# Fourier neural layer with spline network: mixing products over 128 rows, inverse products over 64 rows, and a quarter of the mixing weights loaded one block later

## The chip, the cores and the metric

One NeuronCore of a Trainium2 chip runs the whole kernel in one launch. The metric is the device time of that launch in microseconds; lower is better. All data are fp32.

## What is computed

The input x has 16 images of 64 channels, 128 x 128. It is group-normed (32 groups of two channels), then goes through a spectral convolution plus a 1 x 1 convolution, two layers of a spline network (KAN) over the channels and a GELU, and is added to x:

```python
def spectral_conv2d(x, w1, w2):
    x_ft = jnp.fft.rfft2(x)
    out_ft = zeros((b, c, h, w // 2 + 1), complex64)
    out_ft[:, :, :16, :16]  = einsum('bixy,ioxy->boxy', x_ft[:, :, :16, :16],  w1)
    out_ft[:, :, -16:, :16] = einsum('bixy,ioxy->boxy', x_ft[:, :, -16:, :16], w2)
    return jnp.fft.irfft2(out_ft, s=(h, w))

g = group_norm(x)
y = spectral_conv2d(g, w1, w2) + einsum('bchw,oc->bohw', g, conv_w) + conv_b
y = kan_linear(kan_linear(y as tokens, k1), k2)        # silu product + 8 spline bases
out = x + gelu(y)
```

Only 32 x 16 frequencies of each image are kept (32 values of kx, 16 of ky). Each has its own complex 64 x 64 matrix: w1 and w2 are, as real and imaginary parts, four arrays of 64 x 64 x 16 x 16, 4 MB each.

## The kernel before

The work is done in four blocks; at the end of a block all engines wait for one another, and an engine's program in a block includes what it issues as DMA.

**Forward** (`forward`, L237). For each image TensorE transforms along h (L381), turns the planes (L390) and transforms along w (L402); ScalarE and VectorE evict, and VectorE takes the statistics of the raw image (L355). SP loads the images in eight groups of channels. The kept frequencies of all images stay in SBUF as `modes`: partitions are 64 channels for each of two halves, a half holding eight of the sixteen x of a group. A group g is the lower (w1) or the upper (w2) kx. Behind the last image SP issues the loads of w1's real and imaginary parts (L337, `load_mix_weights`, L133: 8 DMAs of 512 KB a part, in runs of 512 bytes). The buffer `big` has room for all four parts, but w2's parts lie where the images are, so they are issued in the next block.

**Statistics and mixing** (`statistics_and_mix`, L474). SP issues the pick table (L533) and w2's two parts. A chain of small VectorE instructions and three groups of TensorE products gives mean and reciprocal deviation of every image and channel. Then, for both groups g and the eight x of a half: VectorE multiplies the frequencies by the reciprocal deviation into `normed` (two instructions, L664 and L667: -imag, real, imag), TensorE multiplies `normed` by the weights of 16 ky in two parts (L569: 64 products of 64 rows, 32 stationary columns and 64 moving ones, spread over 2 row halves and 4 column tiles), ScalarE evicts (L590), and issues two stores of 128 KB to the scratch `modes_dram` (L595). `normed`, `mixed` and the accumulators have two buffers each. TensorE's program is written out for all 16 x; an fp32 product is two records each of weight load and matmul in the trace. Before a group TensorE waits for its two weight parts (L559).

**Inverse along h** (`inverse_rows`, L673). For each pair of images SP loads the mixed frequencies (`spec`, L705: four DMAs a pair, in runs of 1 KB), TensorE makes 4 products of 512 columns for each of the two images (L756), ScalarE evicts one image and VectorE the other, and SP stores 1 MB of rows for each (L710). Both images of a pair lie in `spec`, in 64 partitions each. The product of one of them runs over all 128 rows, with a table (`inv_h_sb[u]`) whose other 64 rows VectorE has set to zero (L780). SP also loads the first two tiles of the next block here.

**Second half** (`second_half`, L784). 128 tiles of 1024 columns for a pair of images: the inverse along w and the 1 x 1 convolution (L1032, L1040), two spline layers of 14 products each (L1053), with ScalarE and VectorE making their inputs, GELU, and the addition of x by DMA. Tiles run in a loop of two.

The lines that matter most:

```python
for half in range(2):                          # L567, mixing before
    ky, own = col * MIX_Q + at, slice(half * C, (half + 1) * C)
    ins = nc.tensor.matmul(
        ps[u][col * MIX_M:(col + 1) * MIX_M, half, at * C:(at + 1) * C],
        normed[u][own, ky, 1 - part:3 - part, :].rearrange("p r b -> p (r b)"),
        mix_w[g][part][own, :, x, ky], ..., tile_position=(half * C, col * MIX_M))
```

## Time and profile before

| what | value |
|---|---|
| median of 3 runs | 3799.74 us (3797.88 to 3802.43) |
| profiled execution | 3802.58 us |
| its span, first to last instruction | 3800.8 us |
| busy: TensorE, VectorE, ScalarE | 96%, 92%, 89% |
| mean granted TensorE clock | 0.986 |
| DMA | 328.76 MB, 86 GB/s over the span |

The page divides the span into 40 slices of 95 us. Forward fills the first two and most of the third; statistics, mixing and inverse lie in the third to fifth, up to 463 us; the rest is the second half. In the timeline a row is: start in us, us, engine, line, operation, out<-in with shapes, count, and in brackets the idle time of the engine before it with what ended it ("issue": nothing that the profile shows). SPq and ACTq rows are DMA issues.

### The profile page before, as it was taken

Reading aid. Unit: us, or ns where it says so; the run is one execution under the profiler, and the core shown is the slowest. Engines: PE = TensorE matmul, PEld = TensorE weight load, DVE = VectorE, ACT = ScalarE, POOL = GpSimd, SP = SyncE. Lnnn points to the kernel's source line nnn. Section 1 sums busy time; section 2 is a strip of 40 time slices with the busy share of each in tenths; the row PEclk is TensorE's granted clock in tenths of the full one; section 3 lists DMA queues with packets and bytes.
Section 4 is the critical chain, followed back from the end, with each engine's and each line's share of the span. In section 5 each row is a group of like instructions: output and inputs, shape, how many; then the busy total and the mean of one; then the engine's idle time right before and its main releaser. Section 6 shows DMA issues by size and latency. Waiting matters only on the chain.

```text
span 3800.8 us, 103324 instructions
## 1 busy us (share of the span) xinstructions
PE 3658.0 (96%) x38188; PEld 1573.7 (41%) x38188; DVE 3505.1 (92%) x3882; ACT 3391.6 (89%) x3509; POOL 110.8 (3%) x132
## 2 busy tenths in 40 slices
PE   8974699999999999999999999999999999999997
PEld 4433334444444444444444444444444444444444
DVE  7752299999999999999999999999999999999996
ACT  4531299999999999999999999999999999999996
POOL 0000000000000000000000000000000000000000
PEclk9987899999999999999999999999999999999999
DMA  9997723223223223223322322322322322332231
GB/s 260 290 248 140 236 51 72 58 68 72 61 64 72 66 60 72 66 59 72 70 58 69 72 59 67 72 62 64 72 65 60 72 66 59 72 71 58 69 72 45
DMA packets 327425, 328.76 MB, mean 86 GB/s; under 512 B 87120, under 2 KB 259664, under 8 KB 325328
## 3 DMA queue, kind: packets, MB, share of 16 engines
q1 hardware_dynamic: 304336, 256.73, 25.2%
q0 software_dynamic: 18432, 67.12, 10.9%
q10 hardware_dynamic: 4608, 4.20, 0.4%
q8 instruction: 38, 0.62, 0.1%
q14 instruction: 11, 0.09, 0.0%
HBM read 239.88 MB, written 88.08 MB: 86 GB/s over the span
## 4 chain that ended last, share of the span: by engine, by line
PE 86%; DVE 0%; issue 0%; ACT 0%; POOL 0%; POOLq 0%; ACTq 0%; DVEq 0%
PE l_ps L1053 81%; PE y_ps L1040 3%; PE y_ps L1032 3%; DVE cube2l L929 0%; DVE cube3r L929 0%; ACT above L968 0%; ACT offset L983 0%; ACT size L979 0%; ACT S L972 0%; ACT below L976 0%; DVE cube1r L929 0%; DVE cube1l L929 0%; DVE cube0l L929 0%; ACT L972 0%; DVE cube0r L929 0%
## 5 line engine op out<-in xcount | busy, mean ns | idle before, releaser
L983 ACT ACTIVATE offset<-size 128x1024 f32<-128x1024 f32 x1280 | 1240.4, 1044 | 8.2
L929 DVE SCALAR_TENSOR_TENSOR cube0r<-below,offset 128x1024 f32<-128x1024 f32 x256 | 312.4, 1220 | 58.1 <-ACT offset L983 57.5
L929 DVE SCALAR_TENSOR_TENSOR cube0l<-above,offset 128x1024 f32<-128x1024 f32 x256 | 311.5, 1217 | 0.0
L929 DVE SCALAR_TENSOR_TENSOR cube1r<-below,offset 128x1024 f32<-128x1024 f32 x256 | 311.4, 1216 | 0.0
L929 DVE SCALAR_TENSOR_TENSOR cube1l<-above,offset 128x1024 f32<-128x1024 f32 x256 | 311.3, 1216 | 0.0
L929 DVE SCALAR_TENSOR_TENSOR cube3r<-below,offset 128x1024 f32<-128x1024 f32 x256 | 311.3, 1216 | 0.0
L929 DVE SCALAR_TENSOR_TENSOR cube2l<-above,offset 128x1024 f32<-128x1024 f32 x256 | 311.2, 1216 | 0.0
L929 DVE SCALAR_TENSOR_TENSOR cube2r<-below,offset 128x1024 f32<-128x1024 f32 x256 | 311.2, 1216 | 0.0
L938 DVE SCALAR_TENSOR_TENSOR inner_cube<-below,square 128x1024 f32<-128x1024 f32 x256 | 311.2, 1216 | 0.0
L929 DVE SCALAR_TENSOR_TENSOR cube4r<-below,offset 128x1024 f32<-128x1024 f32 x256 | 311.2, 1215 | 0.0
L929 DVE SCALAR_TENSOR_TENSOR cube3l<-above,offset 128x1024 f32<-128x1024 f32 x256 | 311.1, 1215 | 0.0
L929 DVE SCALAR_TENSOR_TENSOR cube4l<-above,offset 128x1024 f32<-128x1024 f32 x256 | 311.1, 1215 | 0.0
L1053 PE MATMUL l_ps<-S,turned_w 64*64 64x512 f32 x2048 | 273.6, 591 | 7.8 <-issue 7.8
L979 ACT ACTIVATE size<-below 128x1024 f32<-128x1024 f32 x256 | 271.2, 1059 | 8.1
L1053 PE MATMUL l_ps<-cube3r,turned_w 64*64 64x512 f32 x2048 | 273.6, 589 | 0.9 <-DVE cube3r L929 0.9
L1053 PE MATMUL l_ps<-cube1l,turned_w 64*64 64x512 f32 x2048 | 273.9, 589 | 0.0
L1053 PE MATMUL l_ps<-cube2l,turned_w 64*64 64x512 f32 x2048 | 273.6, 589 | 0.1
L1053 PE MATMUL l_ps<-cube4r,turned_w 64*64 64x512 f32 x2048 | 273.6, 589 | 0.1
L1053 PE MATMUL l_ps<-cube3l,turned_w 64*64 64x512 f32 x2048 | 273.6, 589 | 0.1
L1053 PE MATMUL l_ps<-cube2r,turned_w 64*64 64x512 f32 x2048 | 273.6, 589 | 0.0
L1053 PE MATMUL l_ps<-cube4l,turned_w 64*64 64x512 f32 x2048 | 273.5, 589 | 0.1
L1053 PE MATMUL l_ps<-cube1r,turned_w 64*64 64x512 f32 x2048 | 273.3, 589 | 0.1
(120 smaller groups left out, 6020.2 us busy)
## 6 DMA issues: line engine op xcount, KB each, us to landing
big<-in_x_dram SPq DMA_DIRECT2D x128, 512.0 KB, 7.0
x_ring<-in_x_dram SPq DMA_DIRECT2D x256, 256.0 KB, 4.0
act_out<-in_x_dram POOLq DMA_DIRECT2D x128, 512.0 KB, 7.1
out_dram<-act_out SPq DMA_DIRECT2D x128, 512.0 KB, 2.7
rows_scratch<-rows SPq DMA_DIRECT2D x16, 1024.0 KB, 6.0
rows_t<-rows_scratch SPq DMA_DIRECT2D x512, 32.0 KB, 5.6
big<-in_spec_w_r_dram SPq DMA_DIRECT2D x16, 512.0 KB, 11.1
big<-in_spec_w_i_dram SPq DMA_DIRECT2D x16, 512.0 KB, 11.1
```

What stands on the lines that cost most here:

```text
L929: nc.vector.scalar_tensor_tensor(out=cube[q][side][:], in0=distance[layer][:], scalar=EDGE - KNOTS[q], in1=offset[layer][q][:], op0=ALU.mi ...
L938: nc.vector.scalar_tensor_tensor(out=inner_cube[:], in0=below[layer][:], scalar=EDGE, in1=square[layer][:], op0=ALU.subtract, op1=ALU.mult ...
L979: nc.scalar.activation(size[layer][:], below[layer][:], ACT.Abs, bias=EDGE, scale=-1.0).then_inc(size_ready[layer], 1)
L983: nc.scalar.activation(offset[layer][q][:], size[layer][:], ACT.Square, bias=-KNOTS[q]).then_inc(offset_ready[layer], 1)
L1032: nc.tensor.matmul(y_ps[image, n * MM:(n + 1) * MM], conv_t[par][half, image], src[half, i * MM:(i + 1) * MM], start=True, stop=False, ski ...
L1040: ins = nc.tensor.matmul(y_ps[image, at:at + W], rows[half, par, h, :], inv_w_sb[half, i, :], start=False, stop=(h == HH - 1), skip_group_ ...
L1053: ins = nc.tensor.matmul(dst[cols, r * MM:(r + 1) * MM], kan_w[layer][rows_, f, :], src[rows_, n * MM:(n + 1) * MM], start=(f == 0), stop= ...
```

## The change

Three parts, with the layouts that go with them.

1. SP issues only w1's real part at the end of the forward block. The imaginary part is issued in the block of statistics and mixing, after the pick table and ahead of w2.
2. A mixing product now reads all 128 rows: `normed` gets a third axis for the half, and the scales `rs_own` and `rs_neg`, zero in the rows of the other half, make the stationary operand (64 columns: two of -imag/real/imag, two halves, 16 images) block-diagonal. There are 32 products for an x, of 128 rows, 64 stationary and 64 moving columns, on two column tiles. VectorE makes `normed` with three multiplies of 512 elements instead of one of 512 and one of 256, and clears the scales once (L610 before). `mixed` gets buffers of its own, and the stores go out in runs of 2 KB instead of 1 KB.
3. In the inverse, one table lies in both halves of the partitions; the product of image u reads only its 64 rows, at tile position (64 u, 0). Nothing is zeroed. `modes_dram` is laid out so that an image's frequencies are loaded in one DMA of 64 rows of 4 KB, two DMAs for a pair.

The tables are permuted to match (columns of `dft_w`, rows of `inv_h`), with the same sizes.

```diff
-            for part in range(2):
-                load_mix_weights(sp, t, weights[:, 2 + part], 0, part)
+            load_mix_weights(sp, t, weights[:, 2], 0, 0)
...
             sp.dma_start(pick_sb[:], t["pick"]).then_inc(pick_loaded, 16)
-            for part in range(2):
-                load_mix_weights(sp, t, mix_w[1][part], 1, part)
+            for g, part in ((0, 1), (1, 0), (1, 1)):
+                load_mix_weights(sp, t, mix_w[g][part], g, part)
...
-                            for col in range(4):
-                                for half in range(2):
-                                    ky, own = col * MIX_Q + at, slice(half * C, (half + 1) * C)
-                                    ins = nc.tensor.matmul(
-                                        ps[u][col * MIX_M:(col + 1) * MIX_M, half, at * C:(at + 1) * C],
-                                        normed[u][own, ky, 1 - part:3 - part, :].rearrange("p r b -> p (r b)"),
-                                        mix_w[g][part][own, :, x, ky], start=(part == 0), stop=(part == 1),
-                                        skip_group_check=True, tile_position=(half * C, col * MIX_M))
+                            for col in range(2):
+                                ky = col * MIX_Q + at
+                                ins = nc.tensor.matmul(
+                                    ps[u][col * C:(col + 1) * C, at * C:(at + 1) * C],
+                                    normed[u][:, ky, 1 - part:3 - part, :, :].rearrange("p f h b -> p (f h b)"), mix_w[g][part][:, :, x, ky],
+                                    start=(part == 0), stop=(part == 1), skip_group_check=True,
+                                    tile_position=(0, col * C))
...
-                        for half in range(2):
-                            n = x + (SH * half if g == 0 else 2 * MODES - SH * (half + 1))
-                            nc.scalar.dma_start(modes_dram[bass.ds(n, 1)].rearrange("n l r b f -> (n l r b) f"),
-                                                mixed[u][:, half, :]).then_inc(stored[u], 16)
+                        for col in range(2):
+                            dst = modes_dram[bass.ds(x + SH * g, 1), :, :, :, col, :]
+                            nc.scalar.dma_start(dst.rearrange("s r h b f -> (s r h b) f"),
+                                                mixed[u][col * C:(col + 1) * C, :]).then_inc(stored[u], 16)
...
-                        nc.vector.tensor_tensor(
-                            normed[u][:, :, 1:3, :].rearrange("p k r b -> p r k b"), here,
-                            rs_signed[:, 0:1, :].unsqueeze(2).to_broadcast([P, 2, MODES, B]), ALU.mult)
-                        nc.vector.tensor_tensor(
-                            normed[u][:, :, 0:1, :].rearrange("p k r b -> p r k b"), here[:, 1:2],
-                            rs_signed[:, 1:2, :].unsqueeze(2).to_broadcast([P, 1, MODES, B]),
-                            ALU.mult).then_inc(normed_ready, 1)
+                        for f, part, scale in ((0, 1, rs_neg), (1, 0, rs_own), (2, 1, rs_own)):
+                            ins = nc.vector.tensor_tensor(
+                                normed[u][:, :, f, :, :], here[:, :, part:part + 1, :].to_broadcast([P, MODES, 2, B]),
+                                scale[:].unsqueeze(1).to_broadcast([P, MODES, 2, B]), ALU.mult)
+                        ins.then_inc(normed_ready, 1)
...
-                    for r in range(2):
-                        at = u * K + r * 2 * MODES
-                        sp.dma_start(spec[p][at:at + 2 * MODES, :].rearrange("n (l f) -> n l f", l=4),
-                                     modes_dram[:, :, r, bass.ds(2 * pair + u, 1), :].rearrange("n l b f -> n l (b f)"))\
-                          .then_inc(spec_loaded[p], 16)
+                    sp.dma_start(spec[p][u * K:(u + 1) * K, :],
+                                 modes_dram[:, :, :, bass.ds(2 * pair + u, 1)].rearrange("s r h b l f -> (s r h) (b l f)"))\
+                      .then_inc(spec_loaded[p], 16)
...
-                            nc.tensor.matmul(ps[u][k][:], inv_h_sb[u][:, part, :], spec[p][:, cols:cols + MM],
-                                             start=True, stop=True).then_inc(rows_done[u], 1)
+                            own = slice(u * K, (u + 1) * K)
+                            nc.tensor.matmul(ps[u][k][:], inv_h_sb[own, part, :], spec[p][own, cols:cols + MM],
+                                             start=True, stop=True, tile_position=(u * K, 0)).then_inc(rows_done[u], 1)
...
-            for u in range(2):
-                other = slice((1 - u) * K, (2 - u) * K)
-                nc.vector.memset(inv_h_sb[u][other], 0.0).then_inc(inv_h_zero, 1)
```

## Rows read from the trace of the kernel before

**Rows 1.** The page: its first line, and the instruction queue's packets, MB, share.
```profile
span 3800.8 us, 103324 instructions
...
q8 instruction: 38, 0.62, 0.1%
```

**Rows 2.** Chain that ended last, second half: start us, us, what.
```profile
575.04 24.03 PE l_ps L1053 x224
...
600.80 24.03 PE l_ps L1053 x224
```

**Rows 3.** Timeline of SP's queue: the weight loads and the pick table.
```profile
239.93 19.46 SPq L141 DMA_DIRECT2D big<-in_spec_w_r_dram  x8
...
259.43 21.56 SPq L141 DMA_DIRECT2D big<-in_spec_w_i_dram  x8
281.63 2.00 SPq L533 DMA_DIRECT2D pick_sb<-pick_dram  x1
...
302.66 22.68 SPq L141 DMA_DIRECT2D big<-in_spec_w_i_dram  x8
```

**Rows 4.** Timeline: first statistics matmuls, two scalings, first mixing matmuls.
```profile
282.10 3.93 PE L541 MATMUL ps_mean<-stats,avg 128*128 128x512 f32 x4 [23.78 <-DVE avg_sq L611]
...
302.27 0.69 DVE L664 TENSOR_TENSOR stats<-modes,rs_signed 128x512 f32<-128x512 f32 x1 [0.33 <-DVE modes L654]
...
302.88 0.42 DVE L667 TENSOR_TENSOR stats<-modes,rs_signed 128x256 f32<-128x256 f32 x1
...
303.56 3.13 PE L569 MATMUL mix_ps<-big,stats 64*32 64x64 f32 x202 [3.05 <-DVE stats L667]
```

**Rows 5.** Windows: length, busy of PE, PEld, DVE, ACT, POOL; PEclk, DMA share, GB/s.
```profile
260.00:270.00 10.00, 0.00 (x0) 0.00 (x0) 0.00 (x0) 0.00 (x0) 0.00 (x0) 0.51 1.21 195
...
332.00:334.00 2.00, 0.00 (x0) 0.00 (x0) 0.00 (x0) 0.00 (x0) 0.00 (x0) 1.00 0.32 89
```

**Rows 6.** Timeline of TensorE while mixing: four of the bursts.
```profile
320.27 2.11 PE L569 MATMUL mix_ps<-big,stats 64*32 64x64 f32 x128 [6.78 <-issue]
...
364.21 2.06 PE L569 MATMUL mix_ps<-big,stats 64*32 64x64 f32 x127 [1.75 <-issue]
...
368.05 2.06 PE L569 MATMUL mix_ps<-big,stats 64*32 64x64 f32 x128 [1.77 <-issue]
...
375.72 1.12 PE L569 MATMUL mix_ps<-big,stats 64*32 64x64 f32 x62 [1.76 <-issue]
```

**Rows 7.** DMA queues from 340 to 376 us: packets, MB, share.
```profile
q8 instruction: 9, 0.15, 2.0%
```

**Rows 8.** Timeline of TensorE: one image's transform along w.
```profile
237.06 2.32 PE L402 MATMUL along_w<-dft_w_sb,freq 128*64 128x64 f32 x70
```

**Rows 9.** Line 595, the stores of mixed frequencies: from issue to landing.
```profile
DMA to landing us min/median/max: 1.7/1.7/8.0
```

**Rows 10.** Timeline of the inverse stage and the second half's first instruction.
```profile
380.51 1.13 SPq L714 DMA_DIRECT2D inv_h_sb<-inv_h_dram  x2
...
386.58 15.68 PE L756 MATMUL rows_ps<-spec,inv_h_sb 128*128 128x512 f32 x32 [9.74 <-DMA spec<-modes_scratch]
...
395.35 1.28 SPq L710 DMA_DIRECT2D rows_scratch<-rows  x2
...
439.35 7.13 PE L756 MATMUL rows_ps<-spec,inv_h_sb 128*128 128x512 f32 x16 [2.31 <-DMA spec<-modes_scratch]
...
454.61 0.91 SPq L710 DMA_DIRECT2D rows_scratch<-rows  x2
...
463.23 0.17 DVE L913 COPY consts<-pair_bias 128x2 f32<-128x2 f32 x1 [8.23 <-PEq L677]
```

**Rows 11.** Windows of the inverse stage, columns as in rows 5.
```profile
386.00:463.00 77.00, 58.45 (x128) 24.39 (x128) 22.13 (x32) 19.11 (x32) 0.00 (x0) 0.94 0.86 282
...
405.00:407.00 2.00, 1.58 (x4) 0.87 (x5) 0.00 (x0) 0.42 (x1) 0.00 (x0) 1.00 1.02 430
```

More of the change, by code:

```diff
@@ L43 @@
 MIX_O = 16
-MIX_M = 2 * B
-MIX_Q = MODES // 4
+MIX_Q = MODES // 2
 PAIRS = B // 2
@@ L66, in tables @@
     c, s = np.cos(aw), np.sin(aw)
-    dft_w = np.stack([np.concatenate([c, -s, c, -s], 1), np.concatenate([-s, -c, s, c], 1)], 1)
+    of_cos = np.stack([c, -s], 2).reshape(W, 2 * MODES)
+    of_sin = np.stack([s, c], 2).reshape(W, 2 * MODES)
+    dft_w = np.stack([np.concatenate([of_cos, of_cos], 1), np.concatenate([-of_sin, of_sin], 1)], 1)
     kx = np.concatenate([np.arange(MODES), np.arange(-MODES, 0)]).astype(np.float64)
+    kx = np.concatenate([kx[:MODES].reshape(2, SH).T.ravel(), kx[MODES:].reshape(2, SH)[::-1].T.ravel()])
     ai = 2 * np.pi * np.outer(kx, h) / H
     inv_h = np.stack([np.stack([np.cos(ai), np.sin(ai)], 1), np.stack([-np.sin(ai), np.cos(ai)], 1)], 1)
-    inv_h = inv_h.transpose(1, 0, 2, 3).reshape(4 * MODES, 2, H)
+    inv_h = inv_h.reshape(MODES, 2, 2, 2, H).transpose(0, 2, 1, 3, 4).reshape(4 * MODES, 2, H)
     weight = np.where(ky == 0, 1.0, 2.0)[:, None] / (H * W)
@@ L125, in first_half @@
         big = sb("big", [P, 4, C * W])
-        rs_signed = sb("rs_signed", [P, 2, B])
+        rs_own = sb("rs_own", [P, 2, B])
+        rs_neg = sb("rs_neg", [P, 2, B])
         mix_loaded = [[ctx.enter_context(nc.semaphore(f"mix_loaded{g}{part}")) for part in range(2)] for g in range(2)]
-        t = dict(t, modes=modes, stats=stats, big=big, rs_signed=rs_signed, mix_loaded=mix_loaded)
+        t = dict(t, modes=modes, stats=stats, big=big, rs_own=rs_own, rs_neg=rs_neg, mix_loaded=mix_loaded)
         forward(nc, t)
@@ L474, in statistics_and_mix @@
 def statistics_and_mix(nc, t):
-    modes, stats, modes_dram, rs_signed, big = (t[n] for n in ("modes", "stats", "modes_dram", "rs_signed", "big"))
+    modes, stats, modes_dram, rs_own, rs_neg, big = (
+        t[n] for n in ("modes", "stats", "modes_dram", "rs_own", "rs_neg", "big"))
     conv_two, conv_bias, image_rs, pair_bias = t["conv_two"], t["conv_bias"], t["image_rs"], t["pair_bias"]
@@ L514, in statistics_and_mix @@
         var_ready, root_ready, chain = sem("var_ready"), sem("root_ready"), sem("chain")
-        rm_ready, bias_done = sem("rm_ready"), sem("bias_done")
+        rm_ready, bias_done, rs_clear = sem("rm_ready"), sem("bias_done"), sem("rs_clear")
         parts = big[:].rearrange("p i (o x k) -> p i o x k", x=SH, k=MODES)
         mix_w = [[parts[:, 2], parts[:, 3]], [parts[:, 0], parts[:, 1]]]
-        NRM, MXD = MODES * 3 * B, 2 * MIX_Q * C
+        NRM = MODES * 3 * 2 * B
         spare = stats[:].rearrange("p b g k -> p (b g k)")
-        normed = [spare[:, u * NRM:(u + 1) * NRM].rearrange("p (k r b) -> p k r b", r=3, b=B) for u in range(2)]
-        mixed = [spare[:, 2 * NRM + u * MXD:2 * NRM + (u + 1) * MXD].rearrange("p (h f) -> p h f", h=2)
-                 for u in range(2)]
-        ps = [ctx.enter_context(nc.psum_tensor(f"mix_ps{u}", [P, 2, MM], F32)) for u in range(2)]
+        normed = [spare[:, u * NRM:(u + 1) * NRM].rearrange("p (k f h b) -> p k f h b", f=3, h=2, b=B) for u in range(2)]
+        mixed = [sb(f"mixed{u}", [P, MIX_Q * C]) for u in range(2)]
+        ps = [ctx.enter_context(nc.psum_tensor(f"mix_ps{u}", [P, MIX_Q * C], F32)) for u in range(2)]
         normed_ready, mix_done, mix_kept = sem("normed_ready"), sem("mix_done"), sem("mix_kept")
@@ L608, in link @@
                 dve.wait_ge(chain, links[0])
+            nc.vector.memset(rs_own[:], 0.0).then_inc(rs_clear, 1)
+            nc.vector.memset(rs_neg[:], 0.0).then_inc(rs_clear, 1)
             nc.vector.memset(avg[:], 0.5 / P).then_inc(set_up, 1)
@@ L650, in _ @@
             link(nc.vector.tensor_scalar(pair_bias[:, :, 1], pair_bias[:, :, 0], EDGE, None, ALU.add))
-            link(nc.vector.tensor_copy(rs_signed[:, 0, :], rs_c[:]))
-            link(nc.vector.tensor_scalar(rs_signed[:, 1, :], rs_c[:], -1.0, None, ALU.mult))
+            dve.wait_ge(rs_clear, 2)
+            for half in range(2):
+                own = slice(half * C, (half + 1) * C)
+                nc.vector.tensor_copy(rs_own[own, half, :], rs_c[own, :])
+                link(nc.vector.tensor_scalar(rs_neg[own, half, :], rs_c[own, :], -1.0, None, ALU.mult))
             dc = modes[0:C, 0, 0, 0, :]
@@ L662, in _ @@
                         dve.wait_ge(mix_done, 2 * x2 + (SH * g + u + 1))
[L663 to L670 removed]
+                        here = modes[:, bass.ds(place_, 1), g, :, :].rearrange("p s (k r) b -> p (s k) r b", r=2)
+                        for f, part, scale in ((0, 1, rs_neg), (1, 0, rs_own), (2, 1, rs_own)):
[3 more added lines that the diff above has]
+                        ins.then_inc(normed_ready, 1)
 def inverse_rows(nc, t):
@@ L685, in inverse_rows @@
         BANKS = 2 * MODES * C // MM
-        inv_h_sb = [sb(f"inv_h_sb{u}", [2 * K, 2, H]) for u in range(2)]
+        inv_h_sb = sb("inv_h_sb", [2 * K, 2, H])
         spec = [sb(f"spec{p}", [2 * K, MODES * C]) for p in range(2)]
@@ L691, in inverse_rows @@
               for u in range(2)]
[L692 removed]
+        inv_h_loaded = sem("inv_h_loaded")
         spec_loaded = [sem(f"spec_loaded{p}") for p in range(2)]
@@ L749, in _ @@
                     pair = 2 * pair2 + p
-                    pe.wait_ge(spec_loaded[p], 64 * (pair2 + 1))
+                    pe.wait_ge(spec_loaded[p], 32 * (pair2 + 1))
                     for k in range(BANKS):
```

9 lines of the change are left out of this document (3 added, 6 removed).

## The prediction

> **What bounds the kernel now.** I read the page first, then the chain of waits, then the timeline stage by stage. The span is 3800.8 us [rows 1]. In the chain of waits the second half is TensorE alone: one tile's products start at 575.04 and the next tile's at 600.80, so 25.76 us a tile, for 128 tiles some 3300 us [rows 2]. The change touches none of that. What it can move is the time at which the second half starts, 463.23 us [rows 10]. Whatever the first 463 us lose or gain arrives at the end one for one, since the chain of the second half holds nothing that was ready earlier. So I look for what ends last in each stage before 463.
>
> *Weights.* SP issues the first weights behind the last images, real part until 259.39, imaginary part until 280.99, each issue some 2.6 us, and only then does the block end: SP's first issue of the next block is at 281.63 and the statistics' first matmul at 282.10 [rows 3, 4]. From 260 on no engine works and the DMA engines run full, 195 GB/s [rows 5]. The second weights are issued until 325.34 [rows 3], and the queue is empty from about 332.5: the stretch 332 to 334 has a DMA share of 0.32 [rows 5]. So the 16 MB of weights are one unbroken stream from 240 to 332.5.
>
> *Mixing.* It starts at 303.56 [rows 4] and ends at 376.84 (375.72 + 1.12), 73.3 us for 16 values of x. But a burst of 128 matmuls, one x, takes only 2.1 us; then TensorE idles with no releaser: 6.78 us before the burst at 320.27, while weights stream, and 1.77 us before that at 368.05, when they don't. Two quiet bursts are 3.84 us apart [rows 6]. The 128 matmul and 128 weight-load records of a burst have a counterpart in the instruction queue: 9 packets, 0.15 MB, in the 36 us from 340 to 376, where some 9.5 bursts fall [rows 7]. So one packet of 16 KB comes for each burst: mixing waits for its own code, at 3.84 us a packet when the DMA is quiet and 8 to 9 us when it is full.
>
> *Inverse.* SP begins it at 380.51; the first product starts at 386.58, the first pair of stores is issued at 395.35, the last at 454.61, and the second half's first instruction follows at 463.23. That is 8.47 us a pair of images (59.26 / 7). The products of one pair take 7.13 us, and TensorE then waits 2.31 us for a spec load [rows 10]. The DMA averages 282 GB/s over the stage but reaches 430 in a stretch that is nearly all stores [rows 11]. So the loop is load, product, store, with DMA and TensorE covering each other only in part.
>
> **The change, part by part.**
>
> *Half of the first weights issued later.* The first block now ends when SP is done with the real part, at about 260, not 281.6. The stream of 32 issues keeps its order, with the pick table between the parts, and stays limited by the DMA: its end stays near 332.5. The imaginary part, 8 issues from about 262 to 283.5, lands near 292 (the last issue of the second weights starts at 325.34 less 2.6 and the queue is empty 10 us later) [rows 3, 5]. The statistics, 21.5 us from 282.10 to 303.56 [rows 4], run from about 260.7 to 282, beside the stream. So mixing of the first group starts at 292 instead of 303.6: it waits for weights, no longer for statistics. SP's only other work that is moved past is the pick table, issued ahead of the imaginary part, 2.00 us [rows 3], needed by VectorE only 8 us later. Two more memsets and two more small VectorE instructions cost under 1 us and lie under that wait for weights: nothing.
>
> *Mixing over 128 rows.* An x has 32 products instead of 64, so 64 matmul and 64 weight-load records: one 16 KB packet of code for two x. This form, 128 rows by 64 columns with 64 moving, exists already: the second transform runs 70 records in 2.32 us, 33 ns each [rows 8], so 64 take 2.1 us. Array work is not saved (half of the stationary operand is zero now); code is. VectorE has three multiplies of 512 elements per x; two in a row start 0.61 us apart, and one takes 0.69 [rows 4], so 1.9 us plus some 0.35 us of signals: 2.3 us an x, beside TensorE. I take 2.3 us an x.
>
> First group: 8 x under the full DMA. Code costs 8.5 / 2 = 4.3 us an x, and the ScalarE stores, which land in up to 8.0 us [rows 9] with two buffers, cost 4 us. The first three x have their code (the first burst now is 202 matmuls [rows 4]), so it ends at about 292 + 7 + 5 x 4.3 = 321. That is before the second weights land, so it is off the path. All 2 MB of its results now go out under the stream, 1 MB more than before, when four of the eight x were done by 332; at the 195 to 280 GB/s of that stretch I add 2.5 us: second weights landed at 335.
> Second group: 8 x 2.3 = 18.4 us. What one packet costs in two x is unseen: nothing if it is fetched beside 4.6 us of work (3.84 is less), 1.77 if not; four packets, 0 to 7 us; I take 1, since the first three x have code waiting. The clock: TensorE idled from 321 to 335, and idle stretches stand at a granted clock of 0.51, the 1.2 GHz level [rows 5]; the slow level on the first x costs 0 to 3 us, I take 2. Mixing ends at 335 + 21.4 = 356.4 instead of 376.8: **20.4 us** gained. Bounds: 332.5 + 17 = 349.5 (27 gained) to 338 + 28 = 366 (11 gained).
>
> *Inverse over 64 rows.* Each image's product reads 64 rows, and the two images of a pair have different row halves. No row shows two 64 x 128 tiles side by side. Lower bound of the products: halved, 3.6 us a pair; upper: 7.13, one after the other. The nearest rows are the second half's 64 x 64 tiles: 8 records in 0.86 us (224 in 24.03) [rows 2], against 0.44 us each (7.13 / 16) for full tiles [rows 10], so four tiles overlap, row halves among them. I take 3.6. Spec loads are 16 issues with 4 KB pieces instead of 32 with 1 KB: same bytes, which relieves SP. The zeroing of unused halves goes; it was hidden by the spec load.
> Then DMA is the bound: 2 MB of stores and 0.5 MB of spec per pair, 2.6 MB, 6.1 us at 430 GB/s (9.3 at the mean of 282, but that has the idle time in it). Turnaround matters: after a spec load lands, products, eviction (1) and latency (about 2) follow, 6.6 us. I take 7.0 us a pair. First store: the first product comes about 1 us earlier, and pair 0, at first at the slow clock, takes 6 us instead of 8.8: 3.8 us less. Seven periods: 7 x 1.47 = 10.3 us less. The two tile loads at the end stay. Together **14 us**. Bounds: 3 (clock at its slow level all through, as TensorE is busy only half of the time, so 7 us a pair again) to 19 (6.2 us a pair and nothing lost).
>
> **Sum:** 20.4 + 14 = 34.4 us. The profiled execution took 3802.58 us (span plus 1.8), so 3768.2; the median of the three runs is 2.8 lower, 3799.74, and gives **3765 us**, 0.9% faster. A difference of 0.2%, 7.6 us, is what a measurement of this kernel can tell from none.
>
> **A rule against it.** The idle of 1.77 us comes once in 256 instructions [rows 6, 7]: that is what the rows show, and the sum goes by it: half of the code, half of the fetches. If the idle belonged to the x instead, the sum would be that of rival 1. The Trainium skill, Runtime: NRT & Kernel Launch, section on instruction fetch mechanics, agrees on blocks of 256 instructions, but says that the cost of crossing one is mostly hidden, since the next is fetched while the current one runs; by that rule the idle has another cause, and halving the code brings nothing. The trace shows the idle, so it does not hide here; which of the two it is, the trace leaves to rival 1.
>
> **Rivals.**
> 1. *The mixing pace stays at 3.84 us an x*, because the idle belongs to the x (buffers, results, stores), not to its code. For it: bursts are also exactly one x. Against it: the first burst of 202 crosses an x without idle [rows 4]. Mixing ends at 335 + 8 x 3.84 = 366; 11 + 14 = 25 us gained: 3775. Chance 0.12.
> 2. *The row halves don't overlap, or the clock drops*: a pair stays at 7 us of TensorE. Inverse gains 3: 23 us in all, 3776. For it: no such tile in the trace, and 0.5 clock levels wherever TensorE idles. Against it: [rows 2]. Chance 0.2; both rivals together, 14 us gained, 3786, chance 0.04.
> 3. *Nothing measurable*: the two stages are held by their transfers after all (weights landing later under 2 MB of stores, stores at 250 GB/s). Gains under 7.6 us: about 3797. Chance 0.03.
> 4. *Slower*: the code after the mixing lies elsewhere in memory, and the second half's loop of two tiles (1056 matmul and weight-load instructions) may no longer be held whole. One fetch a turn at the 1.77 us of [rows 6], 62 turns, is 110 us lost against 34 gained: 3876. It decides from 0.55 us a turn on. Against it: in the whole span the instruction queue moved 38 packets [rows 1], so this loop is fetched once, and its place before was not special. Chance 0.02. The Trainium skill, same page and section, says that a taken branch to a target outside the window forces such a fetch; no run here shows it.
> The forecast itself: 0.59, alone 3757 to 3774.
>
> **Range.** 3752 to 3784: the forecast with its bounds, and rivals 1 and 2. Faster by over 0.2%: 0.94; within: 0.03; slower: 0.03.
>
> **What would show it.** Right: the statistics' first matmul near 261; SP's last weight issue still near 325; the first mixing burst near 292; the second group from about 335 at 2.3 us an x, idle without releaser at most once in two x; mixing done by 357; 64-row products with 3.6 us a pair; DMA share near 1 through the inverse; first instruction of the second half near 429; 25.76 us a tile after it. Wrong: mixing bursts 3.8 us apart per x (1), 7 us of products a pair or a clock of 0.5 in the inverse (2), an idle per turn in the second half (4).

## The result, and the profile after

The changed kernel takes 3785.9 us (median of 6 runs, 3780.91 to 3787.38), beside 3800.87 us for the kernel before in the same 6 rounds: a ratio of 0.9957, 95% interval 0.9947 to 0.9967. It is faster by 15 us, where 35 were forecast, and lies 1.9 us above the range. The profiled execution took 3786.73 us with a span of 3784.9. Each trace below is of one execution.

The second half is what it was: in the chain of waits one tile's products start at 533.50 and the next tile's at 559.27, 25.77 us a tile [rows 2]. So the 15.5 us are all gained before its first instruction, at 447.75 instead of 463.23. Here is SP's queue in the timeline of the changed kernel, and under it the mixing on TensorE:

```profile
259.56 1.99 SPq L539 DMA_DIRECT2D pick_sb<-pick_dram  x1
261.60 18.98 SPq L147 DMA_DIRECT2D big<-in_spec_w_i_dram  x8
280.62 21.82 SPq L147 DMA_DIRECT2D big<-in_spec_w_r_dram  x8
302.48 24.43 SPq L147 DMA_DIRECT2D big<-in_spec_w_i_dram  x8
```

```profile
260.12 3.82 PE L547 MATMUL ps_mean<-stats,avg 128*128 128x512 f32 x4 [2.45 <-DVE avg_sq L618]
...
288.95 21.98 PE L574 MATMUL mix_ps<-big,stats 128*64 128x64 f32 x384 [10.13 <-DMA big<-in_spec_w_i_dram]
...
312.48 7.36 PE L574 MATMUL mix_ps<-big,stats 128*64 128x64 f32 x128 [1.55 <-ACT mixed L595]
...
335.87 28.84 PE L574 MATMUL mix_ps<-big,stats 128*64 128x64 f32 x512 [16.03 <-DMA big<-in_spec_w_i_dram]
```

The block changes at 259.6, the statistics run beside the weights, the last weight is issued at 326.9 (302.48 + 24.43; 325.3 before), and the second group starts at 335.87, when its weights have landed. All of that is as forecast. The new thing is the last row: 512 records in 28.84 us, 56.3 ns each, without a gap. Before, bursts of 16 ns a record stood between idle times [rows 6]; now TensorE is busy all the time at a slower pace, 3.6 us an x instead of 3.84. Mixing ends at 364.71 instead of 376.84.

So the 12.1 us gained there hardly come from the pace of the second group. They come from how much is left when the last weights land. Three more bursts of the kernel before, beside those of [rows 4, 6]:

```profile
311.41 2.08 PE L569 MATMUL mix_ps<-big,stats 64*32 64x64 f32 x127 [4.72 <-issue]
...
328.31 2.13 PE L569 MATMUL mix_ps<-big,stats 64*32 64x64 f32 x127 [5.93 <-issue]
...
334.14 2.08 PE L569 MATMUL mix_ps<-big,stats 64*32 64x64 f32 x128 [3.71 <-issue]
```

Ahead of the burst at 334.14 it had made 202 + 127 + 128 + 127 = 584 records, four and a half x, so eleven and a half were left, 42.7 us of them. The changed kernel has its whole first group done at 319.84 and eight x left, 28.84 us. The code did halve: from 300 to 378 us the instruction queue moved 16 packets (0.26 MB) before, from 286 to 366 us 8 (0.13 MB) after.

The inverse in the same timeline, with four of the seven waits for a spec load, the pairs of stores around them, and the first instruction of the second half:

```profile
375.25 8.87 PE L763 MATMUL rows_ps<-spec,inv_h_sb 64*128 64x512 f32 x32 [10.53 <-DMA spec<-modes_scratch]
...
381.49 0.92 SPq L717 DMA_DIRECT2D rows_scratch<-rows  x2
...
391.43 5.87 PE L763 MATMUL rows_ps<-spec,inv_h_sb 64*128 64x512 f32 x16 [7.32 <-DMA spec<-modes_scratch]
...
398.12 0.87 SPq L717 DMA_DIRECT2D rows_scratch<-rows  x2
...
398.67 3.70 PE L763 MATMUL rows_ps<-spec,inv_h_sb 64*128 64x512 f32 x16 [1.36 <-DMA spec<-modes_scratch]
...
407.98 6.13 PE L763 MATMUL rows_ps<-spec,inv_h_sb 64*128 64x512 f32 x16 [5.61 <-DMA spec<-modes_scratch]
...
414.93 0.88 SPq L717 DMA_DIRECT2D rows_scratch<-rows  x2
...
439.26 0.91 SPq L717 DMA_DIRECT2D rows_scratch<-rows  x2
...
447.75 0.17 DVE L917 COPY consts<-pair_bias 128x2 f32<-128x2 f32 x1 [11.31 <-PEq L685]
```

The products of a pair do take about half of the 7.13 us of [rows 10], 3.70 us, when the clock is up. But every other pair comes after 5.6 to 7.3 us of idle and takes 5.9 to 6.3. The stores of a pair are 8.25 us apart on average ((439.26 - 381.49) / 7), against 8.47. The stage, which starts at 368.98, takes 78.8 us instead of 82.7.

The account of the 15.5 us: mixing 12.1, less 0.6 more between its end and the inverse, inverse 3.95. The last term is the least certain. In e1, e3, e5 and e6 below the inverse is that of the changed kernel, and its stage takes 80.8, 80.8, 81.3 and 79.4 us where this profile has 78.8; with 128-row products it takes 82.7 here, 82.7 in e7 and 82.9 in e9. By these profiles the 64-row inverse is worth 1.4 to 3.95 us.

### The profile page after: what moved, and what is told of

Its sections match the earlier page's. It is cut to its first block, busy times and chain, and to the rows that moved or that the text cites. A ratio compares the mean times of both kernels' runs of the same rounds, so it can differ in the third digit from the quotient of the medians.

```text
span 3784.9 us, 101254 instructions
## 1 busy us (share of the span) xinstructions
PE 3662.3 (97%) x37164; PEld 2765.6 (73%) x37164; DVE 3518.6 (93%) x3900; ACT 3391.7 (90%) x3509; POOL 110.9 (3%) x132
## 4 chain that ended last, share of the span: by engine, by line
PE 87%; DVE 0%; issue 0%; ACT 0%; POOL 0%; POOLq 0%; ACTq 0%; DVEq 0%
PE l_ps L1057 82%; PE y_ps L1044 3%; PE y_ps L1036 2%; DVE cube2l L933 0%; DVE cube3r L933 0%; ACT above L972 0%; ACT size L983 0%; ACT offset L987 0%; ACT S L976 0%; ACT below L980 0%; DVE cube1r L933 0%; DVE cube1l L933 0%; DVE cube0l L933 0%; ACT L976 0%; DVE cube0r L933 0%
## 5 line engine op out<-in xcount | busy, mean ns | idle before, releaser
L1057 PE MATMUL l_ps<-S,turned_w 64*64 64x512 f32 x2048 | 330.5, 592 | 8.1 <-issue 8.1
L1057 PE MATMUL l_ps<-cube1l,turned_w 64*64 64x512 f32 x2048 | 330.0, 589 | 1.0 <-issue 1.0
L1057 PE MATMUL l_ps<-cube0r,turned_w 64*64 64x512 f32 x2048 | 329.9, 591 | 0.6 <-DVE cube0r L933 0.6
L1057 PE MATMUL l_ps<-cube3r,turned_w 64*64 64x512 f32 x2048 | 329.7, 589 | 0.8 <-DVE cube3r L933 0.8
L1057 PE MATMUL l_ps<-below,turned_w 64*64 64x512 f32 x2048 | 329.9, 591 | 0.0
L1057 PE MATMUL l_ps<-cube4r,turned_w 64*64 64x512 f32 x2048 | 329.7, 589 | 0.1
L1057 PE MATMUL l_ps<-cube4l,turned_w 64*64 64x512 f32 x2048 | 329.7, 589 | 0.1
L1057 PE MATMUL l_ps<-bowl,turned_w 64*64 64x512 f32 x2048 | 329.6, 589 | 0.0
L1057 PE MATMUL l_ps<-inner_cube,turned_w 64*64 64x512 f32 x2048 | 329.6, 589 | 0.0
L1057 PE MATMUL l_ps<-cube0l,turned_w 64*64 64x512 f32 x2048 | 329.1, 590 | 0.0
```

The costliest lines, as they stand in the source:

```text
L1057: ins = nc.tensor.matmul(dst[cols, r * MM:(r + 1) * MM], kan_w[layer][rows_, f, :], src[rows_, n * MM:(n + 1) * MM], start=(f == 0), stop= ...
```

## The experiments

Two questions. Why does a mixing record take 56 ns, when the same form takes 33 ns in the transform along w [rows 8]? And why does the inverse hardly gain from half the TensorE time? A third: which part of the change is worth what. The times of the kernels timed in rounds, as ratios to the kernel before in the same job:

| run | median us | ratio, 95% interval |
|---|---|---|
| changed kernel | 3785.9 | 0.9957, 0.9947 to 0.9967 |
| e1 moving operand contiguous | 3778.3 | 0.9938, 0.9921 to 0.9954 |
| e2 loads before stores | 3782.4 | 0.9951, 0.9935 to 0.9968 |
| e3 all of w1 in forward | 3788.9 | 0.9962, 0.9948 to 0.9977 |
| e7 products over 128 rows | 3791.0 | 0.9973, 0.9964 to 0.9983 |
| e8 four spec buffers | 3777.8 | 0.9934, 0.9917 to 0.9951 |
| e9 kernel before, move alone | 3797.7 | 0.9992, 0.9983 to 1.0002 |
| e11 e8, early real products | 3773.1 | 0.9922, 0.9908 to 0.9936 |
| e12 e11, one start flag | 3772.3 | 0.9923, 0.9909 to 0.9936 |

All differences are under 1% of the total. The intervals of e1, e2, e3, e7 and e8 overlap that of the changed kernel, so what sets them apart from it is read from their traces; those of e11 and e12 don't overlap it.

### The pace of the mixing products

**e1**, neighbouring values:

```diff
-  normed[u][:, ky, ...], mix_w[g][part][:, :, x, ky],
+  normed[u][:, ky, ...], big[:, (2 if g == 0 else 0) + part, (x * MODES + ky) * C:(x * MODES + ky + 1) * C],
```

> The changed kernel with one edit: the moving operand of each mixing product is 64 neighbouring values of the weight buffer instead of 64 values 512 bytes apart (other weights, same count, same waits). Theory S (the strided read of the moving operand sets the pace of 56 ns a record): records at about 33 ns as in the transform along w, so an x at 2.1 to 2.3 us instead of 3.6, the second group in 17 to 19 us instead of 28.8, total about 10 us lower, near 3776. Theory C (code fetch still sets the pace, 256 instructions in 7.2 us): unchanged, 28.8 us. Theory W (weight loads of 64 columns over 128 rows do not overlap): unchanged, 28.8 us.

The second group in its timeline:

```profile
335.40 5.52 PE L574 MATMUL mix_ps<-big,stats 128*64 128x64 f32 x128 [17.77 <-DMA big<-in_spec_w_i_dram]
341.19 3.95 PE L574 MATMUL mix_ps<-big,stats 128*64 128x64 f32 x128 [0.27 <-DVE stats L675]
...
349.65 2.08 PE L574 MATMUL mix_ps<-big,stats 128*64 128x64 f32 x64 [0.28 <-DVE stats L675]
352.33 2.24 PE L574 MATMUL mix_ps<-big,stats 128*64 128x64 f32 x64 [0.59 <-ACT mixed L595]
```

An x takes 2.08 us, 32.5 ns a record, and the group 19.2 us. Where it now waits, it waits for VectorE and for ScalarE's evictions. Theory S holds; code fetch and weight loads, which the edit leaves alone, don't set the pace of the second group. The low clock after the idle shows here: granted 0.50 from 335 to 337 and 0.53 from 337 to 339, the first two x take 5.52 us instead of 3.95. Mixing ends 10.1 us earlier, but 2.4 us more pass between its end and the inverse, and the total fell by 7.6 us by the medians.

**e5** and **e6**: is it the power of two, or the step as such?

```diff
-  mix_w[g][part][:, :, x, ky],
+  big[:, ..., x * MODES + ky:x * MODES + ky + 63 * 127 + 1:127],             # e5: 508 bytes
+  big[:, ..., (x * MODES + ky) * 60:(x * MODES + ky) * 60 + 127:2],          # e6: 8 bytes
```

> The changed kernel with the moving values of each mixing product 508 bytes apart instead of 512 (other weights). If the power of two is what slows the strided read: about 33 ns a record, the second group in 17 to 19 us. If any step beyond a short line is slow (the Trainium skill, SBUF - State Buffer, has a note on lines of 16 bytes): unchanged, 56 ns a record and 28.8 us.

> The changed kernel with the moving values 8 bytes apart (other weights). If the step costs as such: 56 ns a record, 28.8 us for the second group. If two values in 16 bytes are enough (same note): as fast as neighbouring values, 33 ns a record, 19 us.

The second group of e5, then of e6 (timelines):

```profile
335.46 30.29 PE L574 MATMUL mix_ps<-big,stats 128*64 128x64 f32 x512 [15.03 <-DMA big<-in_spec_w_i_dram]
```

```profile
336.29 18.54 PE L574 MATMUL mix_ps<-big,stats 128*64 128x64 f32 x512 [15.40 <-DMA big<-in_spec_w_i_dram]
```

508 bytes is as slow as 512 (59 ns a record), 8 bytes as fast as none (36 ns, with the waits). One execution of each gave 3790.6 and 3779.6 us. So it is not the power of two, and not a step as such. That is as far as the runs go: why the far values are slow stays open, and steps between 8 and 508 bytes weren't tried. The Trainium skill, SBUF - State Buffer, section Door 1: The DMA port swizzle, has a note that fits: SBUF is read in lines of 16 bytes, full speed needs two hits in a line. At 8 bytes of step there are two fp32 values in 16 bytes, at 508 one.

Why did the kernel before not show it? It read with the same step. But it had four column tiles and two row halves: a record came every 16.3 ns (2.08 / 128), so each of the eight tiles took one every 130 ns. The changed kernel has two tiles: one every 113 ns each. A contiguous read, e1, gives 65 ns a tile. So I read it thus: the slow stream was there before, hidden behind eight tiles side by side, and with two it sets the pace. This part is not shown; no run reads neighbouring values on eight tiles.

**e4**, the other half of the account: was it code fetch that paced the kernel before? Its imaginary-part products were left out, so that an x has half the code.

```diff
-                        for part in range(2):
+                        for part in range(1):
...
-                                        mix_w[g][part][own, :, x, ky], start=(part == 0), stop=(part == 1),
+                                        mix_w[g][part][own, :, x, ky], start=True, stop=True,
```

> The kernel before with the real-part products of the mixing alone (the imaginary-part products are left out), so 64 matmul and 64 weight-load records an x. Theory C (in the kernel before, one fetch of 256 instructions sets the pace): idle of 1.8 us once in two x, so a quiet x takes about 1.9 us instead of 3.84. Rival X (the idle belongs to the x): idle at every x, a quiet x takes 1.05 + 1.77 = 2.8 us.

```profile
304.12 2.06 PE L569 MATMUL mix_ps<-big,stats 64*32 64x64 f32 x128 [3.05 <-DVE stats L667]
306.53 1.13 PE L569 MATMUL mix_ps<-big,stats 64*32 64x64 f32 x64 [0.35 <-DVE stats L667]
308.08 0.40 PE L569 MATMUL mix_ps<-big,stats 64*32 64x64 f32 x9 [0.42 <-ACT stats L590]
311.02 1.10 PE L569 MATMUL mix_ps<-big,stats 64*32 64x64 f32 x55 [2.54 <-issue]
...
316.88 0.44 PE L569 MATMUL mix_ps<-big,stats 64*32 64x64 f32 x8 [1.31 <-DVE stats L667]
318.47 1.12 PE L569 MATMUL mix_ps<-big,stats 64*32 64x64 f32 x56 [1.15 <-issue]
...
338.90 1.21 PE L569 MATMUL mix_ps<-big,stats 64*32 64x64 f32 x64 [1.68 <-ACT stats L590]
341.01 1.17 PE L569 MATMUL mix_ps<-big,stats 64*32 64x64 f32 x64 [0.89 <-ACT stats L590]
```

The rows to see are x9 and x55. An x has 64 records, and the idle without releaser stands inside it: after 201 records (128 + 64 + 9), as after the 202 of [rows 4], and again 127 later (55 + 64 + 8). The idle belongs to every 128 matmul records, 256 instructions, wherever an x ends. Rival X, and with it rival 1 of the prediction, falls. The number of theory C was missed, and that of rival X nearly hit: a quiet x takes 2.6 us (five steps from 336.05 to 349.08), not 1.9, because ScalarE, which waits for its stores, is late next; once the weights have landed no idle without releaser is left. And in the changed kernel, where a block of 256 instructions lasts 7.2 us, the fetch is hidden whole. So a fetch costs what it takes longer than the work of a block: 3.84 against 2.1 us before.

The same count stands in the first group of e1, beside the full DMA, where an x again has 64 records but of the 128-row form:

```profile
297.78 0.50 PE L574 MATMUL mix_ps<-big,stats 128*64 128x64 f32 x9 [0.24 <-DVE stats L675]
300.03 1.85 PE L574 MATMUL mix_ps<-big,stats 128*64 128x64 f32 x55 [1.74 <-issue]
```

With 192 records ahead of these rows, the idle stands after 201 again, and once more (0.39 us) 127 later. With the strided read gone, the fetch shows again.

### The inverse

**e2**: the spec loads of pair n+2 ahead of the stores of pair n.

```diff
                     for u in range(2):
                         sp.wait_ge(rows_kept[u], BANKS * pair + 2 * BANKS)
-                        store(pair, p, u)
-                    load(pair + 2, p)
+                    load(pair + 2, p)
+                    for u in range(2):
+                        store(pair, p, u)
```

> The changed kernel with SP's order in the inverse turned round: after a pair is evicted, first the spec loads of the pair after next, then the two stores. Theory L (a loop of latencies: a spec load waits in SP's queue behind 2 MB of stores, products wait for it, stores wait for them): the idle of 5.6 to 7.3 us before every other pair's products shrinks below 1 us, a pair takes 6.3 to 7.0 us instead of 8.25, 9 to 13 us less in all, near 3775. Theory B (the DMA moves no more than this mix allows): under 2 us gained.

```profile
384.65 0.97 SPq L717 DMA_DIRECT2D rows_scratch<-rows  x2
...
433.89 0.91 SPq L717 DMA_DIRECT2D rows_scratch<-rows  x2
```

A pair takes 7.03 us ((433.89 - 384.65) / 7), just above what theory L expected. The stage is 5.8 us shorter (370.27 to 443.20, 72.9 us), but by the medians only 3.5 us were gained, a third of what was expected; the second weights landed 1.3 us later in this profile. The first store now waits for both evictions and the loads, and is issued 8.1 us after the first product instead of 6.2, and four of the six later pairs still have 2.4 to 3.8 us of idle ahead of their products. Theory L is supported, but turning the order round isn't the whole remedy.

**e8**: four spec buffers instead of two, the stores first again.

```diff
-            load(0, 0)
-            load(1, 1)
+            for pair in range(4):
+                load(pair, pair)
...
+            for pair in range(PAIRS - 2):
+                for u in range(2):
+                    sp.wait_ge(rows_kept[u], BANKS * pair + 2 * BANKS)
+                    store(pair, pair % 2, u)
+                if pair + 4 < PAIRS:
+                    load(pair + 4, pair)
...
+                    pe.wait_ge(spec_loaded[p], 32 * (pair4 + 1))
```

> The changed kernel with four spec buffers: four pairs are loaded ahead, then the load of pair n+4 is issued behind the stores of pair n. Theory L: products never wait for a spec load after the first, the DMA is the bound at 340 to 380 GB/s, a pair takes 6.5 to 7.2 us instead of 8.25, and the first stores aren't late as in the run with loads ahead of stores: inverse stage 8 to 12 us shorter, total near 3776. Theory B (DMA bound in any case): under 2 us.

Two product bursts in its timeline; then a window over its stage (length; busy time of PE, PEld, DVE, ACT, POOL; PEclk, DMA share, GB/s), and the same view of the changed kernel:

```profile
398.36 5.49 PE L760 MATMUL rows_ps<-spec,inv_h_sb 64*128 64x512 f32 x16 [1.59 <-DVE rows L774]
405.48 3.70 PE L760 MATMUL rows_ps<-spec,inv_h_sb 64*128 64x512 f32 x14 [1.63 <-DVE rows L774]
```

```profile
384.00:436.00 52.00, 31.57 (x104) 14.13 (x100) 16.99 (x27) 14.53 (x27) 0.00 (x0) 0.80 1.02 375
```

```profile
381.00:440.00 59.00, 32.49 (x112) 12.73 (x108) 19.81 (x29) 17.02 (x29) 0.00 (x0) 0.83 0.93 320
```

Products no longer wait for spec but for VectorE's eviction, which waits for its buffer's store: the DMA is the bound, busy throughout (a share of 1.02) at 375 GB/s instead of 320. TensorE's clock still falls at times (0.80 on the mean); with the DMA busy throughout, that is not what sets the pace. A pair takes 6.80 us ((430.49 - 382.90) / 7, the first and the last pair of stores), the stage 69.8 us, 9 less; the total is 8.1 us lower. Theory L holds, theory B for the changed kernel falls.

**e10**: no spec load after the first two pairs, so that later pairs are computed from the frequencies of pairs 0 and 1.

```diff
-                    load(pair + 2, p)
...
-                    pe.wait_ge(spec_loaded[p], 32 * (pair2 + 1))
+                    pe.wait_ge(spec_loaded[p], 32)
```

> The changed kernel without the spec loads after the first two pairs (later pairs are computed from the frequencies of pairs 0 and 1). Theory L: without the load behind the stores, products are never late, and a pair takes what 2 MB of stores take, 4.9 to 5.4 us at 390 to 430 GB/s, instead of 8.25; 20 us less in all, near 3765. Theory B (stores alone are as slow as the mean of the stage, 320 GB/s): 6.5 us a pair or more.

```profile
388.12 3.78 PE L762 MATMUL rows_ps<-spec,inv_h_sb 64*128 64x512 f32 x16 [0.40 <-DVE rows L776]
393.15 3.79 PE L762 MATMUL rows_ps<-spec,inv_h_sb 64*128 64x512 f32 x16 [1.24 <-DVE rows L776]
```

```profile
380.82 24.67 SPq L717 DMA_DIRECT2D rows_scratch<-rows  x12
...
420.52 0.90 SPq L717 DMA_DIRECT2D rows_scratch<-rows  x2
```

From one pair's products to the next 5.04 us pass for 2 MB of stores, 416 GB/s; one execution gave 3768.1 us. Counted as for the others, over all seven steps and so with the two tile loads at the end, a pair takes 5.67 us ((420.52 - 380.82) / 7). So of the 8.25 us a pair in the changed kernel, 5.7 are stores and tile loads, 1.1 come with the spec bytes beside them (e8), and 1.45 are the loop.

**e7**: the changed kernel with products over 128 rows again (two tables, zeroed halves), its loads and layout kept.

```diff
-                            nc.tensor.matmul(ps[u][k][:], inv_h_sb[own, part, :], spec[p][own, cols:cols + MM],
-                                             start=True, stop=True, tile_position=(u * K, 0)).then_inc(rows_done[u], 1)
+                            nc.tensor.matmul(ps[u][k][:], inv_h_sb[u][:, part, :], spec[p][:, cols:cols + MM],
+                                             start=True, stop=True).then_inc(rows_done[u], 1)
```

> The changed kernel with the 64-row products of the inverse undone (two tables with zeroed halves, products over 128 rows), its loads and layout kept. Theory L (a loop of latencies: products of one pair, then stores and the spec load behind them): two pairs take the products' 7.1 to 8 us plus 10 us, 17 to 18 us instead of 16.6, so 2 to 5 us slower than the changed kernel. If the 64-row products were worth what halving them suggests (3.5 us a pair): 20 us or more slower.

5.1 us slower than the changed kernel by the medians. In the profile the stage runs from 368.01 to 450.70, 82.7 us, that of the kernel before: fewer and larger spec loads are worth nothing that shows, and the gain of the inverse, 3.9 us in these two profiles, is that of the 64-row products. In e7 every pair takes 7.13 us of products, the spec load is late by 2.4 to 3.0 us for every other pair, and the clock stays up.

### Which part is worth what

**e3**: all of w1 issued in the forward block again.

```diff
-            load_mix_weights(sp, t, weights[:, 2], 0, 0)
+            for part in range(2):
+                load_mix_weights(sp, t, weights[:, 2 + part], 0, part)
...
-            for g, part in ((0, 1), (1, 0), (1, 1)):
+            for g, part in ((1, 0), (1, 1)):
```

> The changed kernel with the first part of the change undone: both parts of w1 are issued at the end of the forward block again. Theory H (the second weights' landing at about 335 covers the move): the first group starts at 303.5 instead of 289 and ends at about 335 to 338, the second group follows within 3 us of its weights; 0 to 4 us slower, so 3786 to 3790. Rival (the move is worth its 14 us of earlier start): 10 us or more slower, 3796.

```profile
305.65 21.71 PE L575 MATMUL mix_ps<-big,stats 128*64 128x64 f32 x384 [4.09 <-DVE stats L676]
...
332.64 32.42 PE L575 MATMUL mix_ps<-big,stats 128*64 128x64 f32 x576 [1.16 <-ACT mixed L596]
```

The first group starts 17 us later, and mixing ends at 365.06 instead of 364.71. The move gives 0.35 us of mixing in the traces, 3.0 us between the medians, whose intervals overlap; the inverse, which the edit leaves alone, took 2.0 us longer in this profile. Theory H holds: beside the new products the second weights' landing covers the move. The first group, started at 305.65, still makes its x at 3.6 us each beside the full DMA, where the kernel before took 5.8 to 8.9.

**e9**: the kernel before with the move alone (the same lines).

> The kernel before with the first part of the change alone: w1's imaginary part issued in the block of statistics and mixing. Theory C (code fetch sets the pace of its mixing, 8 us an x while weights stream, 3.84 after): the first group starts near 289 instead of 303.5, some seven x are done when the stream ends at 332, the other nine take 35 us: mixing ends at 367 to 369 instead of 376.8, 8 to 10 us faster in all, 3791 to 3794. Rival (the move is worth nothing here too, as under the changed mixing, where it was worth 3 us at most): 3797 to 3801.

```profile
290.86 3.15 PE L568 MATMUL mix_ps<-big,stats 64*32 64x64 f32 x202 [10.56 <-DMA big<-in_spec_w_i_dram]
299.07 2.10 PE L568 MATMUL mix_ps<-big,stats 64*32 64x64 f32 x127 [5.05 <-issue]
...
369.71 1.11 PE L568 MATMUL mix_ps<-big,stats 64*32 64x64 f32 x62 [1.77 <-issue]
```

Mixing starts 12.7 us earlier and ends 6.0 us earlier, at 370.82: the fetches take 6.7 to 8.6 us each for as long as the weights stream, so the early start buys slow x's. The medians differ by 2.3 us, and the interval of the ratio takes in 1. That is less than theory C's 8 to 10 us and inside the rival's 3797 to 3801; by the one trace it is not nothing. So the worth of the move alone stays open between the two.

### A version that beats both

In the changed kernel TensorE idles for 16 us ahead of the second group, though the real part of the second weights has long landed. **e11** takes the version of e8 and makes the real-part products of the group's first two x (there are two buffers) before the wait for the imaginary part. With a start flag on the first product of each 64 columns, these two x lost early sums; the last section has the rule that fits. **e12** sets the flag on the first early product of a bank and column tile alone.

```diff
+                for x in early:                        # x = 0, 1 of the second group
+                    pe.wait_ge(normed_ready, SH * g + x + 1)
+                    pe.wait_ge(mix_kept, SH * g + x + 1)
+                    for at in range(MIX_Q):
+                        products(x, at, 0, first=(at == 0))     # e11: start flag for every at
+                pe.wait_ge(t["mix_loaded"][g][1], 32 * (C // MIX_O))
```

> The kernel with four spec buffers, and in the second group the real-part products of the first two x are made before the wait for the imaginary part, in the 15 us in which TensorE idles. Their 3.6 us leave the path: mixing ends at about 361 after weights at 335, total 3 to 4 us under the kernel with four buffers alone, near 3774. If the second group is bound by something else than TensorE's products: no gain.

> The run before (four spec buffers, real-part products of two x ahead of the wait), with the start flag on the first early product of a bank and column tile alone, so that the real and imaginary parts of all columns are summed. Same instructions otherwise: the same time, 3771 to 3776, mixing done about 26 us after the second weights land instead of 28.8.

The mixing of e12 around the second weights' landing:

```profile
318.81 1.98 PE L568 MATMUL mix_ps<-big,stats 128*64 128x64 f32 x32 [1.26 <-ACT mixed L606]
321.52 1.99 PE L568 MATMUL mix_ps<-big,stats 128*64 128x64 f32 x32 [0.72 <-ACT mixed L606]
331.94 3.83 PE L568 MATMUL mix_ps<-big,stats 128*64 128x64 f32 x64 [8.44 <-DMA big<-in_spec_w_i_dram]
336.12 21.64 PE L568 MATMUL mix_ps<-big,stats 128*64 128x64 f32 x384 [0.35 <-DVE stats L686]
```

The group is done 25.8 us after its weights (357.76 - 331.94) instead of 28.8. e12 takes 3772.3 us, 0.77% under the kernel before and 13.6 us under the changed one. The difference to e8, 5.5 us by the medians, is more than the 3 us that the trace explains; in this profile the weights also landed 4.7 us earlier than in that of e8 (331.94 for 336.67), though the edit leaves their DMAs alone.

## Why the prediction was wrong

**Right.** The second half takes no part, and every gain comes before it. The block changes at 260; SP's stream ends where it did (326.9); the first group, forecast from 292 to 321, runs from 289 to 320 (its end by luck: forecast as code under the full DMA at 4.3 us an x, it is the strided read at 3.7); the second group's start, forecast at 335, is 335.87. The mixing before was paced by its code, a packet for 256 instructions (e4), and with half the code the first group is off the path. Two 64-row tiles of 128 columns do overlap: 3.70 us a pair, forecast 3.6. The last stores of the inverse to the second half take 8.5 us, as before.

**The step that failed first:** "the second transform runs 70 records in 2.32 us, 33 ns each [rows 8], so 64 take 2.1 us. [...] I take 2.3 us an x." The row has the same tile, the same shape and the same type, but a contiguous moving operand. The weights are read 512 bytes apart, and such a record takes 56.3 ns on two column tiles (e1, e5). The group takes 28.84 us instead of 21.4, a term short by 7.4 us. The row of the old mixing seemed to say that the step costs nothing, 16 ns a record; as I read it, eight tiles shared the cost. With 28.84 for 21.4, a start at 335.87 instead of 335, mixing ends at 364.71 for the forecast 356.4; of the 20.4 us, 12.1 came. Of the 2 us put in for the clock at most 0.4 show: the first x after the idle, which is evicted at 339.80, takes 3.9 us, the others 3.5 to 3.7 from one eviction to the next; the strided read hides the rest, since without it (e1) the low clock costs 1.6 us.

**The second:** "I take 7.0 us a pair." It took DMA as the bound. The turnaround was named, but with the spec load landed at its start; what wasn't counted is that a load stands in SP's queue behind 2 MB of stores. From a store's issue to the landing of the load behind it and the next products 9.9 us pass (398.12 to 407.98), then 7 us of products at the low clock and eviction until the next store (414.93): 16.8 us, in which two pairs fit, 8.4 us a pair. TensorE's share of that loop is what was halved, and idling for 5.6 to 7.3 us took its clock from 2.4 to 1.2 GHz, so that the pair that matters takes 5.9 to 6.3 us instead of 7.13, not 3.7. A window within such a pair's products, then one within products of e7 (columns as in [rows 5]):

```profile
391.00:393.00 2.00, 1.57 (x4) 0.85 (x6) 0.00 (x0) 0.00 (x0) 0.00 (x0) 0.50 1.01 426
```

```profile
393.00:395.00 2.00, 1.93 (x5) 0.98 (x6) 0.00 (x0) 0.60 (x1) 0.00 (x0) 1.00 1.04 438
```

e7, with 128-row products, keeps 1.00 in every window of 2 us from 381 to 445. With 8.25 for 7.0, seven times, 8.8 us of the 14 are gone; the first store came 2.3 us earlier, forecast 3.8. That the bound was within reach e8 shows: 6.80 us a pair with two more buffers.

**Rivals.** Rival 1's cause is refuted (e4), though its end of the mixing, 366, is close to the truth, by another mechanism. Rival 2 named half of the truth for the inverse, the clock, and priced it at 3 us gained; 3.95 came. Its other half, tiles that don't overlap, is not so. The combined price of the two, 3786, which had a chance of 0.04, is the measured 3785.9; that is luck, since rival 1's cause is refuted and of rival 2 only the clock came. Both stages came out near the bad end of the bounds set for them (12.1 of 11 to 27, 3.95 of 3 to 19), while the sum took both near the good end, and the range left out their coming together.

**The rule that spoke against the change.** The Trainium skill, Runtime: NRT & Kernel Launch, section on instruction fetch mechanics, calls the cost of a block boundary mostly hidden. In the kernel before it is not hidden (1.77 us once in 256 instructions, and up to 6.8 us beside a full DMA), so the trace does not agree there; in the changed kernel it is hidden.

## What to carry to other kernels

A duration taken from another line's row is good only if the access pattern is the same too: a matmul record with its moving values 512 bytes apart took 1.7 times as long as one that reads neighbours, on two column tiles; with eight tiles a record came every 16 ns in spite of it. When an engine's work in a loop of load, compute and store is halved, follow one buffer round the loop through the queue it waits in before taking the bandwidth for the bound; two more buffers (e8) gave more than halving the products did. And a transfer that starts earlier is worth next to nothing where the next one's landing, in the same stream, ends last (e3). Last, when two terms of a sum are both taken near their good ends, the range has to hold what comes out if neither holds.

## What the runs showed of the hardware

- The moving operand's step: 32.5 ns a record of 128 x 64 contiguous, 56.3 ns at 512 bytes, 59 at 508, 36 at 8 bytes with waits, on two column tiles.
- TensorE waits for code when a block of 256 instructions runs in less time than its fetch takes: 3.4 to 3.9 us on a quiet DMA, 6.7 to 8.9 us beside a full one (8.6 in e9: from 299.07 to 307.65 to 316.24). Where the block lasts 7.2 us at most 0.99 us of it shows (e11, beside the weights).
- A start flag on each early product loses sums that are open in other columns of its bank; e12, which differs from e11 in that flag alone, keeps them. The Trainium skill, PSUM - Partial Sum Buffer, section The four PSUM rules, says so: the flag clears the accumulate bits of the whole bank in the quadrants that it writes.
- Less work for TensorE can make it slower at what is left: 128-row products kept the full clock (e7), the 64-row ones of the changed kernel ran at half of it after each wait of 5.6 to 7.3 us (5.9 to 6.3 us a pair) and at the full clock after those of 0.9 to 1.4 us (3.70 us).
